# Where the gates are worked out, how the conditioned rows are copied, when the down weights load and where the warm stream stands, in a fused conditioning and expert FFN kernel

## The reference

```python
w = weights[conditions]
xf = jnp.einsum('bct,bcd->bdt', x, w).reshape(2048, 512)
gate = jax.nn.softmax(jnp.einsum('nh,eh->ne', xf, Wr), axis=-1)
top2_val, top2_idx = jax.lax.top_k(gate, 2)
rank = (jnp.cumsum(onehot, axis=0) * onehot).sum(-1)
w_assign = jnp.where(rank <= 640, flat_val, 0.0)
g = jax.nn.silu(jnp.einsum('nh,eih->eni', xf, Wg))
u = jnp.einsum('nh,eih->eni', xf, Wu)
out_e = jnp.einsum('eni,ehi->enh', g * u, Wd)
x = x + jnp.einsum('ne,enh->nh', comb, out_e)
```

## Time and profile before

| | us |
|---|---|
| runs | 290.47, 289.10, 289.03 |
| median | 289.1 |
| profiled execution | 288.85 |
| its span | 287.0 |
| mean granted clock, of full speed | 0.982 |

### The profile page before, as it was taken

The page is one execution under the profiler, slowest core; times in us unless marked ns, Lnnn a source line. Parts: engine busy times, 40 slices in busy tenths (PEclk is TensorE's granted clock), DMA queues, the critical chain, the costliest instruction groups (busy, mean ns, idle before and its releaser), DMA issues.

```text
span 287.0 us, 4871 instructions
## 1 busy us (share of the span) xinstructions
PE 275.1 (96%) x1735; PEld 237.9 (83%) x1736; DVE 126.4 (44%) x256; ACT 127.9 (45%) x213; POOL 164.3 (57%) x150
## 2 busy tenths in 40 slices
PE   8999799999999999999999999999999999999990
PEld 4663339989999999999999999999999999999970
DVE  1658945433353345444353443354335544442210
ACT  2347914444444455444544444444445545533320
POOL 5790068332387575776445558675758568573232
PEclk9999869999999999999999999999999999999997
DMA  6995989999389787858676659787977765644536
GB/s 207 374 315 207 380 203 366 303 393 371 97 108 242 167 198 183 177 138 167 138 186 138 154 138 224 134 169 197 181 163 197 187 136 81 127 80 50 69 39 73
DMA packets 28913, 53.50 MB, mean 186 GB/s; under 512 B 7200, under 2 KB 7328, under 8 KB 28896
## 3 DMA queue, kind: packets, MB, share of 16 engines
q0 software_dynamic: 10576, 21.67, 41.6%
q1 hardware_dynamic: 18320, 31.60, 32.6%
HBM read 32.74 MB, written 20.25 MB: 185 GB/s over the span
## 4 chain that ended last, share of the span: by engine, by line
PE 93%; DVE 2%; ACT 1%; issue 1%; POOLq 1%; POOL 1%
PE bank L997 47%; PE bank L1018 25%; PE bank L979 5%; PE bank L1029 4%; PE bank L854 3%; PE bank L965 2%; PE bank L866 2%; PE bank L916 2%; PE bank L877 1%; PE bank L910 1%; PE bank L959 1%; POOLq L83 1%; POOL out L498 1%; PE bank L899 1%; ACT tiles L525 0%
## 5 line engine op out<-in xcount | busy, mean ns | idle before, releaser
L498 POOL DMA_INDIRECT out<-tiles,dst_row x40 | 64.9, 1623 | 34.0 <-DMA out<-tiles,dst_row 13.2
L997 PE MATMUL bank<-whi,xhi 128*128 128x352 f32 x280 | 70.7, 333 | 0.8 <-ACT xhi L571 0.8
L486 POOL DMA_INDIRECT gate_g<-gates_dram,src_row x40 | 41.9, 1047 | 51.5 <-ACT tiles L588 44.8
L997 PE MATMUL bank<-wlo,xhi 128*128 128x352 f32 x280 | 67.7, 323 | 0.0
L806 DVE TENSOR_TENSOR xlo<-bank,xhi 128x512 fp32r<-128x512 f32 x35 | 24.2, 692 | 77.2 <-ACT xhi L571 77.2
L476 POOL DMA_INDIRECT tiles<-xf_dram,src_row x40 | 41.0, 1025 | 27.7 <-DVE dst_row L797 15.8
L997 PE MATMUL bank<-whi,xlo 128*128 128x352 f32 x280 | 56.6, 323 | 0.0
L997 PEld LDWEIGHTS bank<-whi,xhi 128*128 128x128 f32 x280 | 48.0, 189 | 4.2 <-issue 1.4
L997 PEld LDWEIGHTS bank<-wlo,xhi 128*128 128x128 f32 x280 | 48.8, 188 | 0.0
L571 ACT ACTIVATE xhi<-bank 128x512 fp32r<-128x512 f32 x35 | 20.9, 597 | 58.7 <-PE bank L979 58.7
L997 PEld LDWEIGHTS bank<-whi,xlo 128*128 128x128 f32 x280 | 47.0, 189 | 0.0
(11 more groups left out here) (99 smaller groups left out, 237.8 us busy)
## 6 DMA issues: line engine op xcount, KB each, us to landing
raw<-wgu SPq DMA_DIRECT2D x32, 352.0 KB, 4.4
x_sb<-x SPq DMA_DIRECT2D x8, 512.0 KB, 7.8
raw<-wd SPq DMA_DIRECT2D x8, 512.0 KB
out<-x_sb SPq DMA_DIRECT2D x4, 1024.0 KB, 9.0
xf_dram<-tiles SPq DMA_DIRECT2D x7, 512.0 KB, 3.3
raw<-wd SPq DMA_DIRECT2D x8, 192.0 KB
out<-x_sb SPq DMA_DIRECT2D x1, 1280.0 KB, 15.2
tiles<-xf_dram,src_row POOLq DMA_INDIRECT x40, 4.5
```

The lines of the kernel that those rows point to most:

```text
L486: nc.gpsimd.indirect_dma_start(out=gate_g[:, n % TPE, :], out_offset=None, in_=gates_dram[:, :], in_offset=bass.IndirectOffsetOnAxis(ap=sr ...
L498: nc.gpsimd.indirect_dma_start(out=out[:, :], in_=y_sb[:, n % TPE, :], in_offset=None, out_offset=bass.IndirectOffsetOnAxis(ap=dst_row[:, ...
L997: last = nc.tensor.matmul(ps[:, 0:I], left[:, b, c], right[:, half, o:o + I], start=(k == 0 and left is xhi and right is whi), stop=(k == ...
```

## The change

- `exps` and `gates` are no longer in two halves. ScalarE takes one exponent of all tiles behind the first rounding of weights, and VectorE works out all gates behind the lists and the weights' low parts. The first `subtract` moves behind `one_hot(1)` and covers 14 tiles; `one_hot(0)` moves ahead of the last `xr_sum`.
- SyncE stores the gates behind the landing of the first gather.
- ScalarE's 16 `xf_copy` follow one another; the first rounding of weights (`W0_EARLY`) comes behind them.
- The first expert's down weights are loaded right behind its gate and up weights, ahead of the stores of conditioned rows.
- `condition(2)` is cut in two: one half ahead of the last `turn`, one behind the logits. Of the others one stands ahead of the rank, not two, and five behind it, not four.
- The warm stream is 8 matmuls ahead of the picks (into a PSUM bank that `subtract` has read) and 14 behind, instead of 18 behind.

```diff
-BEFORE_RANKS = 4
-GATED = 2 * LG[1][1]
-EARLY_PAIRS = 2
-KEEP_WARM = 18
+AHEAD_OF_PICKS = 8
+KEEP_WARM = 14
 # SyncE
-            for u in range(KH):
+            for u in range(NU):
                 load_unit(0, u)
...
-            sp.wait_ge(gates_ok, 2)
+            sp.wait_ge(xg_in[0], 16)
+            sp.wait_ge(gates_ok, 1)
             sp.dma_start(gates_dram.rearrange("(j p) e -> p j e", p=P),
                          gate[:, :, :]).then_inc(gates_out, 16)
-            load_unit(0, KH)
-
-            sp.wait_ge(xg_in[0], 16)
 # ScalarE
-            for n in range(2):
+            for n in range(XR):
                 xf_copy(n, n)
-            exps(0)
-            for n in range(2, XR):
-                xf_copy(n, n)
+            with act.Fori(1, TT // XR) as i:
+                for s in range(XR):
+                    xf_copy(i * XR + s, s)
             for u in range(W0_EARLY):
                 w_high(u, 0, 0)
...
+            act.wait_ge(sub_ok, 2)
+            nc.scalar.activation(ex[:, :, :], lg[:, :, :], ACT.Exp).then_inc(ex_ok, 1)
 # VectorE
-            subtract(0, GATED)
+            dve.wait_ge(consts, RANKS)
             xrT_copy(NM - 1)
             xr_sum(NM - 2)
-            gates(0)
+            one_hot(0)
             xr_sum(NM - 1)
-            dve.wait_ge(consts, RANKS)
-            one_hot(0)
             top_two(2)
             top_two(3)
-            subtract(GATED, LG[3][0] * 2)
             subtract(LG[3][0] * 2, TT)
             one_hot(1)
-            gates(1)
+            subtract(0, LG[3][0] * 2)
...
             for u in range(W0_EARLY, KH):
                 w0_low(u)
+            gates()
 # TensorE
-            condition(2)
+            condition(2, (0,))
             turn(NM - 1)
             logits(2)
             logits(3)
-            after = EARLY_PAIRS * 2 + BEFORE_RANKS
-            for j in range(EARLY_PAIRS * 2, after, 2):
-                condition(j)
+            condition(2, (1,))
+            condition(4)
...
-            for j in range(after, TT, 2):
+            for j in range(6, TT, 2):
                 condition(j)
...
             pe.wait_ge(consts, CONSTS)
+            pe.wait_ge(sub_ok, 2)
+            keep_warm(AHEAD_OF_PICKS, bank[4])
             pe.wait_ge(what_ok, 1)
...
-            for _ in range(KEEP_WARM):
-                nc.tensor.matmul(ps_hT[:, :], iota_q[:, 0:P // AQ, :]
...
+            keep_warm(KEEP_WARM, ps_hT)
```

More of the change, by code:

```diff
@@ L901, in logits, with condition @@
                 last.then_inc(lg_ps, 1)
-            def condition(j):
+            def condition(j, qs=(0, 1)):
                 if j >= XR:
                     pe.wait_ge(xf_ok, j - XR + 2)
-                for q in (0, 1):
+                for q in qs:
                     for n in (j, j + 1):
@@ L911, in condition @@
                                                 x_sb[rows, n, :], start=True, stop=True)
-                last.then_inc(xf_ps, 2)
+                if 1 in qs:
+                    last.then_inc(xf_ps, 2)
             pe.wait_ge(warm_clear, 1)
@@ L950, in _, with keep_warm @@
             last.then_inc(rank_ps, 1)
-            for j in range(after, TT, 2):
+            for j in range(6, TT, 2):
                 condition(j)
+            def keep_warm(n, ps):
+                for _ in range(n):
+                    nc.tensor.matmul(ps, iota_q[:, 0:P // AQ, :].rearrange("p q a -> p (q a)"),
+                                     iota_q[:, 0:H // AQ, :].rearrange("p q a -> p (q a)"),
+                                     start=True, stop=True)
             pe.wait_ge(consts, CONSTS)
+            pe.wait_ge(sub_ok, 2)
+            keep_warm(AHEAD_OF_PICKS, bank[4])
             pe.wait_ge(what_ok, 1)
```

28 lines of the change are left out of this document (6 added, 22 removed).

## The result

| | before | changed |
|---|---|---|
| runs, us | 290.47, 289.10, 289.03, 288.93, 290.07 | 291.18, 293.84, 293.86, 293.74, 293.79 |
| median, us | 289.1 | 293.8 |
| profiled execution, us | 288.85 | 291.18 |
| its span, us | 287.0 | 289.4 |

The ratio is 1.0135, 95% interval [1.009, 1.018]: slower, where I had forecast 288.2 and a range up to 290.0. Medians are of all runs; a ratio compares only runs within 1.5% of the fastest run of the same kernel.

The account below looks back on a forecast made before the run. TensorE's packed stream was taken as the bound, its start overshooting the first gather's data by 0.8 us. Lists 1.0 and stores 0.7 us later, gather landing 0.6 quicker: first turn 0.9 us earlier, 288.2 us, range 286.8 to 290.0.

Parts of the forecast that it names:

- The half condition: TensorE ahead of the last turn: half of condition(2) moved behind the logits brings the turn about 0.5 us earlier.
- The copies: ScalarE's copies of conditioned rows, with five conditions behind the rank: they end about 0.8 us later, bounds 0 to +1.0.
- The stores: Stores of conditioned rows on a full DMA queue: last landing near 37.4 against 36.7, +0.7 us, from -0.3 to +0.9.
- The warm stream ahead of the picks: Eight TensorE matmuls take 1.7 us: picks start at 34.6, lists come 1.0 us later at 37.3, second part ends at 40.1.
- The faster pace: TensorE's picks, no longer fed by VectorE: an estimated 53 ns each could end them 0.8 us sooner; not in the sum.
- The gather: GpSimd's first gather, behind stores and lists: issued at 37.95, landing in 3.2 us instead of 3.8, data at 41.15.
- The gap: TensorE ahead of the first turn: free at 40.1, before the data, instead of 42.09; idle about 1 us expected.
- Slower rival: Clock drops before or within the warm stream's first part: 2.7 us lost, 291.8 us; chance 0.10, whole or in part.
- Gates' store, late gates and the queues behind them: SyncE and GpSimd: gates' store issued near 41.2, gates gathered 1 to 2 us later, still covered ahead of their first reader.
- It does not do what it says: Rival: stores and lists hold the gather until 38.8, it lands near 42, nothing changes, 289.0 us; chance 0.13.

Follow-up runs that it names:

- f2: Changed kernel with condition(2) in one piece again ahead of the last turn: 290.8 us, ratio 1.0044 to the kernel before.
- e8: Changed kernel with TensorE's order of before, all 14 warm matmuls behind the picks; other engines' edits stay: 295.2 us, ratio 0.994 to the kernel before.
- e5: Changed kernel run again, nothing altered: 298.4 us, ratio 1.0109 to the kernel before.
- e2: Changed kernel with the first expert's down weights loaded behind the stores of conditioned rows again: 298.8 us, ratio 1.0108 to the kernel before.
- e1: Changed kernel with 28 instead of 14 warm matmuls behind the picks: 298.9 us, ratio 1.0139 to the kernel before.
- e6: Changed kernel with no warm matmuls ahead of the picks and 22 behind: 298.7 us, ratio 1.0109 to the kernel before.
- g2: Changed kernel, nothing altered, 12 runs on another chip: 292.8 us, ratio 1.0095 to the kernel before.
- e9: Changed kernel a third time, nothing altered: 299.5 us, ratio 1.007 to the kernel before.
- f3: Changed kernel once more, nothing altered, on the chip of f1 and f2: 295.6 us.
- e4: Kernel before with 14 instead of 18 warm matmuls behind the picks: 296.0 us against 296.2, ratio 0.998.
- e10: Kernel before against itself, nothing altered, on one of the later chips: 296.3 us, ratio 0.9954.
- g1: f1 with 22 instead of 14 warm matmuls behind the picks: 289.2 us, ratio 0.9997 to the kernel before.
- f1: Changed kernel with the conditions in the order of before, 8 warm matmuls still ahead of the picks, 14 behind: 289.8 us, ratio 1.0017 to the kernel before.
- e3: Changed kernel with condition(6) also ahead of the rank, four conditions behind it instead of five: 297.8 us, ratio 1.0124 to the kernel before.

## Why the prediction was wrong, step by step

Two terms carry most of the miss. The last store's landing stood in the sum with 3.4 us and took 4.7. TensorE's idle ahead of the first turn stood in it at no price, and the clock that fell behind it cost 1.6 us. The first term's cause is open; the steps below follow the prediction's own order.

**The half condition failed.** "Half goes behind the logits, so the turn comes about 0.5 us earlier" took matmuls to be additive. `quadrants` puts a condition's two pairs on different row halves of the array, and they ran side by side: two matmuls (x4) took 1.08 us where four (x8) had taken 1.09. The turn's load again stood 0.81 us and came at R + 1.94, against 1.96. The Trainium skill (TensorE: Matmul & The Clock Gate, Part 3: Packing small matmuls) says that matmuls on different row groups run at the same time in one array; 1.08 against 1.09 agrees. I had not applied it to an edit that takes away one of two such tiles. So the rank gained 0.17 us from R, not 0.6. It gains 0.15 with condition(2) whole (f2, e8), so this is VectorE's shorter queue, which I had at 0.1. The rank's time in the trace, 26.61, lay near my 26.5 only since R was 0.35 us early.

**The copies were right in mechanism and size**: one more condition behind the rank costs a wait. Last copy R + 12.71 against 11.48, +1.23. I had +0.8, with a rank 0.46 us earlier from R than it came; the two errors are the same 0.4 us.

**The stores were half right.** I had the last landing at R + 15.6. In e5 and f2 it came at 15.9 and 16.3. In four of the five profiles of the changed kernel it came at 17.4 to 17.7, since the last store took 4.7 to 4.9 us. This term I had as 3.4 from one row, and let the landing move by 0.9 us at most; from R it moved by 2.5 in the first profile. The DMA engines' share is 0.06 from 37.5 to 38.0 and 0.05 to 38.5, close to one engine of sixteen, and 0.00 from 38.5 on. The other four late landings show the same share of 0.06; one engine's part was still under way when the others had ended. The Trainium skill (DMA: Bandwidth & Descriptors, Why a DMA increments its semaphore by 16 and not by 1) says that a transfer counts as landed only when each engine's share has; the gather's wait to 38.83 agrees. The lag was in 5 of the 10 profiles whose last copy ends at R + 12.3 or later, and in none of the 8 with the last copy near 11.4. e2, whose down weights stood late, had 3.5, but e1, e5, e6 and f2 were quick with them early.

One record goes with it in every profile. In the five late ones a 16 KB packet of the instruction queue starts at R + 6.1, while the stores fill the DMA engines, and takes 1.6 to 1.9 us. In twelve quick ones it starts at R + 3.6 to 4.1, and in the last, f2, at R + 6.9 and takes 0.9. In e5 it starts at R + 3.7, near the end of the down weights, and all other engines then stand idle until R + 6.0, so the one could catch up. The queues of the changed kernel from 27.0 to 29.5 us:

```profile
q1 hardware_dynamic: 397, 0.78, 81.5%
q8 instruction: 1, 0.02, 4.0%
```

A packet that holds one engine for 4.0% of sixteen engines' 2.5 us, or 1.6 us, would leave that engine behind by about what the landing is late. That is a lead and not a shown cause: no run moved the packet, and why it starts at R + 6.1 in some executions is open.

**The warm stream ahead of the picks was right**: picks at 34.56 (34.6 predicted), lists 37.37 (37.3), second part over at 40.15 (40.1). That these agree to a tenth is in part luck. From R all three are 0.3 to 0.4 us later than predicted, as the copies are, and the early R hides it. The picks' own pace held as well: 2.57 us for 32 with all inputs there and the clock at 1.00, 0.080 each. The faster pace that I had estimated, 53 ns a pick, was seen in no run.

**The gather**: the 0.8 us between its last condition and its issue stayed, 0.75 in every profile, where I took a quarter of a microsecond off. Its landing took 3.42 us against 3.8, but that gain is not shown by the other profiles: 3.77 in g2, and from issue to the turn's load 3.9 to 4.1 in e5, e9, f3 and g2 against 4.0 in e4. I had taken 3.2. Data came at 43.0, not 41.15. From R the turn came 2.3 us later than my sum: 0.3 from the copies, 1.4 to 1.5 from the last store's landing, and the rest from the gather's start and landing.

**The gap was taken as harmless; beside the late landing this step cost most, 1.6 us.** I wrote that the second part ends before the data and counted this as gained. TensorE's idle of about 1 us ahead of the first turn stood in my list as a sign of being right, at no price. It was 2.98 us. I looked for a fall of the clock within the warm stream, and put the Slower rival there. The fall came behind the stream. Behind a gap of 2.0 us or more ahead of the first turn the clock fell in 9 of 11 profiles, and the two turns behind it came 1.3 to 2.8 us late (9.36 to 10.80 against 8.04). With a gap of 1.1 or less it fell there in none of seven. The earlier trace rows had the hint: 1.51 us of idling ahead of the picks and a fall behind it. The profiles bear it out: of the six that idle 1.5 us ahead of the picks five have a fall in the picks or the warm stream behind them (not e4), and of the 12 that come to the picks with at most 0.1 us of idling none has. So the picks alone do not bring it. In the kernel before, the fall hits warm matmuls, which lose nothing that anyone waits for, and makes the 18 last longer: 6.59 us in the profile before. They do not always cover the landing. In e10 the clock was low for half as long, the 18 took 5.27 us, the landing was late, and TensorE waited 1.09 us.

**Gates' store, late gates and the queues behind them** were right: the store was issued at 43.02, 1.8 us later than predicted with the gather, and `y_scale` did not wait for the gates: TensorE released it in every profile.

**The chances.** "It does not do what it says" (stores and lists hold the gather, data near 42) describes the first half of what happened; the clock then came on top. I held these as separate cases, at 0.13 and 0.10, though the first makes the gap that brings the second. That is why neither the range nor its upper end held the result. The upper end, 290.0, was the sum of no mechanism.

## To carry to other kernels

A wait just ahead of dense TensorE work has two prices: its own length and the clock that may fall behind it, so a warm stream is better sized to a late landing than to the median one. The traces say so (g1 against f1); the times here do not separate the two, and 28 matmuls in e1 were too many. Before a TensorE step is cut in two, look whether its parts already run side by side on different rows; half of such a step costs the whole. Two fillers that each fit the same idle stretch don't both fit it (lists at R + 14.5 with either, 15.95 with both), so a change with several moves is added up on the resource they share.

## What the hardware showed that I had not expected

- Two 64-row matmuls of 512 columns took 1.08 us and four of them, on both row halves, 1.09.
- Gaps of 2.0 to 3.7 us were enough for the clock to fall to 1.2 GHz, in most executions and not in all (e4, 2.37 us, and e5, 2.06 us, kept it). It stayed low about 3 us in seven cases and 6 to 7 in two (e9, f1).
- One DMA engine can end well behind the others at the end of a queue that had been full: the last store landed in 3.2 to 3.7 us or in 4.7 to 5.1, never between, and the late ones go with an instruction packet in the full stretch.
- GpSimd's first indirect gather starts 0.75 us after the last store's landing, in all 18 profiles; a gather that waits for nothing starts after 0.30.
- TensorE can stand for up to 5.5 us in the first 17 us of the same program, on some chips and not on others, and again for up to 2.4 us near 60 us. In 10 of the 11 profiles with the early stall the clock fell there too (not in e3). The traces don't tell what stops it.
